# One group of small products moved from the middle of a layer to the border between two layers, in a fused delta-rule attention and MLP kernel

## The chip, the cores and the metric

The kernel runs on one core of one Trainium2 chip. The metric is the device time of one execution in microseconds (us); lower is better. Engines are called by the names that the profile gives them: PE is TensorE (matmuls), PEld its weight loads, DVE VectorE, ACT ScalarE, POOL GpSimd, SP the engine that issues most DMAs.

## The reference

For 4 sequences of 2048 tokens with 256 features the kernel computes one block with adaptive layer norm. Its first half is a gated delta rule in chunks of 64 tokens, its second half an MLP with ternary weights. Cut to what matters:

```python
h = layernorm(x) * (1 + ca) + sa
# attention: per head (4 heads, 64 wide), per chunk of 64 tokens, S is the state carried on
A     = inv(eye - A0)                    # A0 from keys x keys, strictly lower triangular
v_new = A @ v - (A @ wk) @ S             # the new values: "keys times old state" is in here
o     = rk_g @ S + intra @ v_new
S     = gamma_C * S + wk_g @ v_new
x = x + ga * (h + (alpha * o) @ Wr.T)
h = layernorm(x) * (1 + cb) + sb
h = silu(h @ w1.T * s1) * (h @ w2.T * s2)    # 256 -> 1024
h = gelu(h @ h1.T * s) ; h = gelu(h @ h2.T * s)   # 1024 -> 1024, twice
x = x + gb * (h @ w3.T * s3)                 # 1024 -> 256
```

All inputs and outputs are float32.

## The kernel before

**Tiling.** The state S ties the 32 chunks (`STEPS`) of a sequence together, so the kernel walks over chunks and treats all four sequences at once: a tile has 64 tokens of two sequences on its 128 partitions and the other pair beside them, 256 tokens in all (`TOK`). The MLP keeps features on the partitions and the 256 tokens along the free axis; its layers are called l1 (w1 and w2, 8 column blocks), l2 and l3 (the two 1024x1024 ones, 8 column blocks each, 16 matmuls per block), and y (w3). All weights stay on the chip. Activations are split into a high and a low part, which are multiplied with the same weights, one after the other (`act_hi`, `act_lo`; `xh`, `xl`).

**The attention's pieces** of one chunk, as names of the schedule: "start" (transposes of the normed tokens and keys), "values" (tokens times Ww), "gram" (keys times keys), "fs" and "expand" (the inverse of small blocks, VectorE), "pred" (keys times old state, for v_new), "u" (VectorE: values minus that product), "lead" (inverse times u, and queries times the old state), "join", "state" (the new state), "attn_out". Between attention and MLP of the same chunk stand "norm2" (VectorE: the second norm, tile `xn2`), "turn" (TensorE: transposes of `xn2`), "ln2" (ScalarE) and "parts" (VectorE: high and low part).

**What sets the order.** There is no scheduler. Lists written by hand give the order in which every engine meets the pieces: `alone` and `opening` for the first step, `second` and `third` for the next two, and `mixed` for steps 3 to 33 (of which 24 run in a hardware loop of 12 unrolled steps). Each engine walks the same list (`walk`, line 364) and issues, at each name, what this engine has to do for it. A name in the list thus sets a place in the queue of every engine that has code for it. Engines synchronise by semaphores that are waited for in front of the instruction.

A step n of `mixed` works on several chunks: l3 and y belong to step n-1, l1 and l2 to the chunk of step n, and an entry with 1 or 2 as its third number to a chunk ahead (`a = n + ahead`). So the order within a step is: transposes for the next chunk, l3 with its insertions, y, l1, "lead", l2 with its insertions.

**The lines that matter here.**
- TensorE, "pred" (lines 1318 to 1327, matmul L1325): for 4 pairs of sequence and head pair, 2 halves of the tokens and 2 heads, one product of a 64x64 block of the turned keys `rT` with a 64x64 block of `state`: 16 matmuls, each on a quarter of the array, into the columns 0 to 255 of both banks of `duo[0]`. It waits for the constants and for `hT_ready` and `rT_ready` of the chunk ahead (`begun`, line 384), since the transposes of that chunk lie in `duo[0]` until ScalarE and VectorE have copied them out.
- VectorE, "u" (lines 932 to 936): `v[p]` minus that product, written to `v[p]`; it sets `u_ready`, for which "lead" waits (line 1388).
- TensorE, "gram" (L1316, also 16 products on quarters of the array, into `duo[1]`), "values" (L1304, full array), "turn" (L1440, four transposes on the full array; it waits for `xn2_ready`, line 1437).
- TensorE, y (`last_layer`, L1235) and l1 (`layer`, L1163). The first l1 block waits for `xl_ready` and for VectorE's reading of `mlp[0]` (`y_mid[0]`, line 1177), the second for that of `mlp[1]` (line 1179).
- "lead" (L1136, L1142, then L1129, L1120) and "state" (L1420, L1422): groups of small products on quarters of the array, between l1 and l2 and inside l2.

Of the kernel before, what the change touches and what calls it, by code (L numbers as in the profile page):

```python
# [1 line left out]

# [104 lines left out]
def adaln_block(nc, x, wts, wv, wr, wmod, cT, scales, s3, decay, const, out):  # L107
    with ExitStack() as ctx:
        def sb(name, shape, dt=F32, c=ctx):
            return c.enter_context(nc.sbuf_tensor(name, [P] + list(shape), dt))  # L110

        def sem(name):
            return ctx.enter_context(nc.semaphore(name))

        def sems(name, n):
            return [sem(f"{name}{i}") for i in range(n)]

        main(nc, ctx, sb, sem, sems, x, wts, wv, wr, wmod, cT, scales, s3, decay, const, out)


def main(nc, ctx, sb, sem, sems, x, wts, wv, wr, wmod, cT, scales, s3, decay, const, out):
# [88 lines left out]
    gram = sb("gram", [2, NP, C])  # L210
    intra = [sb(f"intra{i}", [2, NP, C]) for i in range(2)]
# [28 lines left out]
    y = sb("y", [NB, D])  # L240
# [43 lines left out]
    def listed(first, columns, between):  # L284
# [4 lines left out]

    mixed = listed([("rg", 0, 0), ("start", 0, 1)], late + layers[:2 * HK], {  # L290
        ("l3", 0): [("norm2", 0, 0)],
        ("l3", 1): [("values", 0, 1), ("pred", 0, 0), ("gram", 0, 1), ("turn", 0, 0), ("intra", 0, 1), ("u", 0, 0)],
# [6 lines left out]
        ("l1", 7): [("lead", 0, 0), ("far", 0, 1), ("stats", 0, 2)],  # L299
        ("l2", 0): [("old", 0, 0), ("norm", 0, 2)],  # L300
        ("l2", 1): [("keys", 0, 0)],
# [1213 lines left out]
```

## Time and profile before

| | |
|---|---|
| median of 3 runs | 1745.33 us (1743.48 to 1747.3) |
| profiled execution, span from its first to its last instruction | 1742.3 us |
| profiled execution, its own device time | not given apart from the span; the three runs stand 1.2 to 5.0 us above the span |
| TensorE matmuls busy | 1716.0 us, 98% of the span |
| VectorE, ScalarE, GpSimd busy | 64%, 55%, 34% |
| HBM traffic | 18 GB/s over the span |

The span is what the trace covers; a run's time has the launch and the end in it as well. A matmul's "busy" time overlaps with that of the next (each lasts 0.28 us by the trace and the next starts 0.11 us later), so on TensorE it is the distance between starts that tells how fast work is issued. In the timelines a row can stand for several instructions of one line in a row (xcount); its time is the start of the first. Float32 products on quarters of the array leave two records each, so a group of 16 products is a row of x32.

### The profile page before, as it was taken

What the parts mean: (1) busy time and instruction counts of PE and PEld (TensorE: products, weight loads), DVE (VectorE), ACT (ScalarE), POOL (GpSimd) and SP (SyncE); (2) the same over time, 40 slices, a digit from 0 to 9 for tenths busy, and PEclk for the clock granted to TensorE, in tenths of its full rate; (3) what the DMA queues carried; (4) which work ended last, traced back from release to release, by engine and by line L of the source; (5) the groups of instructions that cost most, each with busy time, mean ns of one, the idle gap of its engine ahead of it and who ended that gap; (6) DMA issues with size and microseconds to landing.
All of it is one profiled execution on the core that took longest, in us unless ns stands there. A gap on an engine that the chain in (4) does not pass through costs nothing.

```text
span 1742.3 us, 60528 instructions
## 1 busy us (share of the span) xinstructions
PE 1716.0 (98%) x25488; PEld 1651.6 (95%) x25488; DVE 1115.4 (64%) x3041; ACT 963.3 (55%) x2249; POOL 593.5 (34%) x694
## 2 busy tenths in 40 slices
PE   8799999999999999999999999999999999999999
PEld 5698999999999999999999999999999999999998
DVE  5677666666666666676666676666666666666432
ACT  4664555555555555555555555555555555565554
POOL 3544333343333343333243333243233243243101
PEclk8899999999999999999999999999999999999999
DMA  8101000000000000000000000000000000000000
GB/s 291 68 14 33 12 23 23 18 20 11 24 23 23 18 20 11 24 23 24 17 21 15 20 23 23 20 17 19 16 23 23 21 17 21 14 23 17 8 3 12
DMA packets 37356, 47.08 MB, mean 27 GB/s; under 512 B 9236, under 2 KB 29336, under 8 KB 37080
## 3 DMA queue, kind: packets, MB, share of 16 engines
q1 hardware_dynamic: 35088, 40.75, 8.4%
q8 instruction: 206, 3.38, 0.8%
q10 hardware_dynamic: 1992, 2.38, 0.5%
q14 instruction: 70, 0.57, 0.1%
HBM read 22.53 MB, written 8.39 MB: 18 GB/s over the span
## 4 chain that ended last, share of the span: by engine, by line
PE 93%; DVE 1%; issue 1%; POOL 1%; ACT 1%; DVEq 0%; POOLq 0%
PE mlp L1163 64%; PE mlp L1235 6%; PE solo L1163 3%; PE duo L1431 3%; PE solo L1304 3%; PE solo L1136 2%; PE duo L1352 1%; PE duo L1129 1%; PE duo L1420 1%; PE solo L1440 1%; PE duo L1124 1%; PE duo L1325 1%; PE solo L1146 1%; PE duo L1422 1%; PE duo L1316 1%
## 5 line engine op out<-in xcount | busy, mean ns | idle before, releaser
L1163 PE MATMUL mlp<-act_hi,w_hi 128*128 128x256 f32 x4096 | 968.0, 283 | 1.1 <-POOL act_lo L668 0.6
L1163 PE MATMUL mlp<-act_lo,w_hi 128*128 128x256 f32 x4096 | 945.2, 277 | 0.0
L1163 PEld LDWEIGHTS mlp<-act_hi,w_hi 128*128 128x128 f32 x4096 | 770.1, 188 | 9.8 <-POOL act_lo L668 1.3
L1163 PEld LDWEIGHTS mlp<-act_lo,w_hi 128*128 128x128 f32 x4096 | 770.4, 188 | 0.8
L805 ACT ACTIVATE full<-mlp,scale_sb 128x256 f32<-128x256 f32 x512 | 246.4, 481 | 553.7 <-PE mlp L1163 553.5
L895 DVE TENSOR_TENSOR act_lo<-full,act_hi 128x256 fp32r<-128x256 f32 x512 | 240.2, 469 | 321.7 <-ACT act_hi L806 319.1
L668 POOL TENSOR_TENSOR act_lo<-full,act_hi 128x256 fp32r<-128x256 f32 x256 | 186.6, 735 | 501.9 <-ACT act_hi L795 501.9
L806 ACT ACTIVATE act_hi<-mlp,scale_sb 128x256 fp32r<-128x256 f32 x512 | 242.6, 474 | 0.0
L1163 PE MATMUL mlp<-xh,w_hi 128*128 128x256 f32 x768 | 190.8, 286 | 3.5 <-issue 3.0
L1163 PE MATMUL mlp<-xl,w_hi 128*128 128x256 f32 x768 | 189.8, 282 | 0.0
L607 POOL TENSOR_TENSOR rstd<-ve,minus_half 128x2 f32<-128x2 f32 x64 | 49.1, 768 | 331.7 <-DVE ve L844 331.3
L1014 DVE SCALAR_TENSOR_TENSOR full<-mlp,scale_sb,gate 128x256 f32<-128x256 f32 x192 | 92.8, 484 | 99.2 <-ACT gate L790 96.8
L1163 PEld LDWEIGHTS mlp<-xh,w_hi 128*128 128x128 f32 x768 | 145.9, 190 | 5.1 <-issue 4.2
L790 ACT ACTIVATE gate<-mlp,scale_sb 128x256 f32<-128x256 f32 x192 | 91.0, 474 | 107.7 <-PE mlp L1163 107.7
L1163 PEld LDWEIGHTS mlp<-xl,w_hi 128*128 128x128 f32 x768 | 146.2, 190 | 0.0
L1235 PE MATMUL mlp<-w_hi,act_hi 128*128 128x256 f32 x512 | 118.2, 277 | 0.0
L1235 PE MATMUL mlp<-w_hi,act_lo 128*128 128x256 f32 x512 | 118.1, 276 | 0.0
L607 POOL TENSOR_TENSOR rinv<-ssm,minus_half 128x8 f32<-128x8 f32 x32 | 52.8, 1650 | 182.2 <-DVE ssm L873 182.2
L795 ACT CAST act_hi<-full 128x256 fp32r<-128x256 f32 x256 | 101.7, 397 | 10.6 <-DVE full L1014 10.6
L1235 PEld LDWEIGHTS mlp<-w_hi,act_hi 128*128 128x128 f32 x512 | 96.1, 188 | 0.1
L1235 PEld LDWEIGHTS mlp<-w_hi,act_lo 128*128 128x128 f32 x512 | 96.1, 188 | 0.0
L779 ACT ACTIVATE h<-solo,sbm,cb 128x64 f32<-128x64 f32 x256 | 84.0, 438 | 0.3 <-PE solo L1440 0.3
(179 smaller groups left out, 2679.9 us busy)
## 6 DMA issues: line engine op xcount, KB each, us to landing
w_raw<-in_wts SPq DMA_DIRECT2D x22, 512.0 KB, 5.0
kg<-r SPq DMA_DIRECT2D x64, 126.0 KB
xin<-in_x SPq DMA_DIRECT2D x62, 128.0 KB
out_y<-y SPq DMA_DIRECT2D x62, 128.0 KB, 2.5
step_and_inv<-square_t SPq DMA_DIRECT2D x56, 64.0 KB, 2.0
wmod_sb<-in_wmod ACTq DMA_DIRECT2D x1, 1024.0 KB, 9.1
kg<-last SPq DMA_DIRECT2D x64, 2.0 KB
last<-r SPq DMA_DIRECT2D x64, 2.0 KB, 1.7
```

Source lines behind the costliest of these rows:

```text
L607: pool.tensor_tensor(dst[:], src[:], minus_half[:, 0:src.shape[1]], ALU.pow).then_inc(done, 1)
L668: pool.tensor_tensor(act_lo[0][:, k, :], full[k % 3][:], act_hi[0][:, k, :].bitcast(F32), ALU.subtract).then_inc(l_ready[0], 1)
L779: ins = act.activation(h2[:].rearrange("p k b n -> p (k b n)")[:, cols], solo[1][:, cols], ACT.Identity, bias=sbm[:, k, b:b + 1], scale=cb ...
L790: act.activation(gate[k % 2][:], gated[k % 3][:, 0:TOK], ACT.Silu, scale=scale_sb[:, 0, k:k + 1]).then_inc(l_act[0], 1)
L795: act.copy(act_hi[0][:, j, :], full[j % 3][:]).then_inc(l1_hi, 1)
L805: act.activation(full[k % 2][:], mlp[k % 2][:, 0:TOK], ACT.Gelu, scale=s)
L806: act.activation(act_hi[layer % 2][:, k, :], mlp[k % 2][:, 0:TOK], ACT.Gelu, scale=s).then_inc(l_act[layer], 1)
L895: dve.tensor_tensor(act_lo[layer % 2][:, k, :], full[k % 2][:], act_hi[layer % 2][:, k, :].bitcast(F32), ALU.subtract).then_inc(l_ready[la ...
L1014: dve.scalar_tensor_tensor(full[k % 3][:], up, s, gate[k % 2][:], ALU.mult, ALU.mult).then_inc(prod_ready, 1)
L1163: mm = pe.matmul(dst, *general_ops, start=is_first and i == 0, stop=is_last and i == 1)
L1235: mm = pe.matmul(mlp[k][:, 0:D], *ops, start=j == 0 and i == 0, stop=j == HK - 1 and i == 1)
L1304: mm = pe.matmul(solo[0][:, b * D:(b + 1) * D], hT[:, kt, b, :], wv_sb[:, kt, :], start=kt == 0, stop=kt == KT - 1)
```

## The change

One list is edited. In `mixed`, "pred" and "u" leave the place behind l3's second column and stand at the end of what follows l3's last column, behind both halves of y and so in front of l1. The lists of the first three steps are as before. The file also lost 15 blank lines at its top: line L1325 of before is L1310 of after, and so on for all.

```diff
     mixed = listed([("rg", 0, 0), ("start", 0, 1)], late + layers[:2 * HK], {
         ("l3", 0): [("norm2", 0, 0)],
-        ("l3", 1): [("values", 0, 1), ("pred", 0, 0), ("gram", 0, 1), ("turn", 0, 0), ("intra", 0, 1), ("u", 0, 0)],
+        ("l3", 1): [("values", 0, 1), ("gram", 0, 1), ("turn", 0, 0), ("intra", 0, 1)],
...
-        ("l3", 7): [("parts", 0, 0), ("silu", 0, 0), ("y", 0, 0), ("y", 1, 0)],
+        ("l3", 7): [("parts", 0, 0), ("silu", 0, 0), ("y", 0, 0), ("y", 1, 0), ("pred", 0, 0), ("u", 0, 0)],
```

TensorE at the old place, before: values (L1304), pred (L1325, `state` and `rT`), gram (L1316), turn (L1440), then l3's third column.

```order
L1163 MATMUL mlp<-act_lo,w_hi 128x256
L1300 REGISTER_ALU
L1304 MATMUL solo<-wv_sb,hT 128x256 x4
L1325 MATMUL duo<-state,rT 64x64 x16
L1316 MATMUL duo<-rT 64x65 x16
L1440 MATMUL solo<-con,xn 128x128 x4
L1163 MATMUL mlp<-act_hi,w_hi 128x256
```

The same place after the change (line numbers 15 lower):

```order
L1148 MATMUL mlp<-act_lo,w_hi 128x256
L1285 REGISTER_ALU
L1289 MATMUL solo<-wv_sb,hT 128x256 x4
L1301 MATMUL duo<-rT 64x65 x16
L1425 MATMUL solo<-con,xn 128x128 x4
L1148 MATMUL mlp<-act_hi,w_hi 128x256
```

The 16 products of pred are gone from between values and gram.

TensorE at the border from y (L1235) to l1 (L1163 with `xh` and `xl`), before:

```order
L1235 MATMUL mlp<-w_hi,act_hi 128x256
L1235 MATMUL mlp<-w_hi,act_lo 128x256
L1163 MATMUL mlp<-xh,w_hi 128x256
L1163 MATMUL mlp<-xl,w_hi 128x256
L1163 MATMUL mlp<-xh,w_hi 128x256
```

And after the change:

```order
L1220 MATMUL mlp<-w_hi,act_hi 128x256
L1220 MATMUL mlp<-w_hi,act_lo 128x256
L1310 MATMUL duo<-state,rT 64x64 x16
L1148 MATMUL mlp<-xh,w_hi 128x256
L1148 MATMUL mlp<-xl,w_hi 128x256
```

The 16 products, on quarters of the array, now stand between two layers on the full array.

VectorE at the same border, before: the two halves of y (L1024, L1026) and the first product of l1 (L1014):

```order
L1024 TENSOR_TENSOR y<-mlp,mods 128x256
L1026 TENSOR_TENSOR y<-y,x_0 128x256
L1024 TENSOR_TENSOR y<-mlp,mods 128x256
L1026 TENSOR_TENSOR y<-y,x_0 128x256
L1010 ISA
L1014 SCALAR_TENSOR_TENSOR full<-mlp,scale_sb,gate 128x256
```

And after, with u (L921, was L936):

```order
L1009 TENSOR_TENSOR y<-mlp,mods 128x256
L1011 TENSOR_TENSOR y<-y,x_0 128x256
L1009 TENSOR_TENSOR y<-mlp,mods 128x256
L1011 TENSOR_TENSOR y<-y,x_0 128x256
L921 TENSOR_TENSOR v<-v,duo 128x2x4x64
L995 ISA
L999 SCALAR_TENSOR_TENSOR full<-mlp,scale_sb,gate 128x256
```

The subtraction has moved behind the two halves of y; it stood behind "intra" (L930) before. ScalarE, GpSimd and SP have the same order before and after.

## Rows read from the trace of the kernel before

**Rows 1.** the page's head and its part 1, busy time of each engine
```profile
span 1742.3 us, 60528 instructions
...
PE 1716.0 (98%) x25488; PEld 1651.6 (95%) x25488; DVE 1115.4 (64%) x3041; ACT 963.3 (55%) x2249; POOL 593.5 (34%) x694
```

**Rows 2.** waits, whole run; columns: engine, line, awaited, us in total, times, longest
```profile
PEld duo L1325 <- issue: 9.6, 29, 0.3
...
PE solo L1440 <- DVE xn L1000: 2.2, 2, 1.9
```

**Rows 3.** all waits of TensorE from 230 to 1600 us
```profile
PE duo L1120 <- issue: 0.7, 2, 0.4
PE mlp L1163 <- issue: 0.3, 1, 0.3
```

**Rows 4.** one period: busy us by engine, then clock, DMA share, GB/s
```profile
1000.00:1052.00 52.00, 52.00 (x798) 50.60 (x797) 34.42 (x94) 28.95 (x70) 18.06 (x21) 1.00 0.08 20
```

**Rows 5.** TensorE's timeline, lead; start, length, line, operation, xcount [idle before]
```profile
1032.73 0.28 PE L1163 MATMUL mlp<-xl,w_hi 128*128 128x256 f32 x1
1032.94 0.27 PE L1136 MATMUL solo<-v,diag 64*64 64x64 f32 x2
...
1033.04 0.23 PE L1136 MATMUL solo<-v,diag 64*64 64x64 f32 x2
...
1033.10 0.22 PE L1136 MATMUL solo<-v,diag 64*64 64x64 f32 x2
```

**Rows 6.** TensorE's timeline, small groups inside the second layer
```profile
1046.24 0.69 PE L1420 MATMUL duo<-intra,vn 64*64 64x64 f32 x32
1046.75 0.65 PE L1422 MATMUL duo<-vn,kg 64*64 64x64 f32 x32
1047.33 0.38 PE L1163 MATMUL mlp<-act_hi,w_hi 128*128 128x256 f32 x1
1047.55 0.28 PE L1163 MATMUL mlp<-act_lo,w_hi 128*128 128x256 f32 x1
```

**Rows 7.** TensorE's timeline, the old place
```profile
1009.05 0.69 PE L1325 MATMUL duo<-state,rT 64*64 64x64 f32 x32
1009.57 0.65 PE L1316 MATMUL duo<-rT 64*64 64x65 f32 x32
1010.15 0.66 PE L1440 MATMUL solo<-con,xn 128*128 128x128 f32 x4
```

**Rows 8.** TensorE's timeline, the new place
```profile
1025.06 0.28 PE L1235 MATMUL mlp<-w_hi,act_lo 128*128 128x256 f32 x1
1025.17 0.28 PE L1163 MATMUL mlp<-xh,w_hi 128*128 128x256 f32 x1
1025.29 0.28 PE L1163 MATMUL mlp<-xl,w_hi 128*128 128x256 f32 x1
```

**Rows 9.** TensorE's timeline, turn in step 31
```profile
1632.37 0.66 PE L1440 MATMUL solo<-con,xn 128*128 128x128 f32 x4
```

**Rows 10.** VectorE's timeline, same step, and step 31
```profile
1007.59 1.79 DVE L1000 SCALAR_TENSOR_TENSOR xn<-x,mv,rstd 128x256 f32<-128x256 f32 x2
...
1011.64 0.68 DVE L936 TENSOR_TENSOR v<-v,duo 128x512 f32<-128x512 f32 x1
...
1025.83 0.42 DVE L1026 TENSOR_TENSOR y<-y,x 128x256 f32<-128x256 f32 x1
1026.83 0.48 DVE L1014 SCALAR_TENSOR_TENSOR full<-mlp,scale_sb,gate 128x256 f32<-128x256 f32 x1 [0.58 <-ACT gate L790]
...
1631.36 0.87 DVE L1000 SCALAR_TENSOR_TENSOR xn<-x,mv,rstd 128x256 f32<-128x256 f32 x2
```

**Rows 11.** TensorE's timeline, the new place in another step
```profile
817.13 0.32 PE L1163 MATMUL mlp<-xh,w_hi 128*128 128x256 f32 x1
817.29 0.28 PE L1163 MATMUL mlp<-xl,w_hi 128*128 128x256 f32 x1
```

## The prediction

> **What bounds the kernel now.** I read the page's first part first: TensorE's matmuls are busy for 98% of the span, the next engine (VectorE) for 64% [rows 1]. Then the waits: over the whole run TensorE waited twice, 2.2 us in all, for the normed tokens `xn`, the operand that stands next to the moved work [rows 2]; but from 230 to 1600 us, which is the steady loop, its waits are 0.7 + 0.3 = 1.0 us altogether, none of them on another engine [rows 3]. A stretch of 52.00 us, one period, has it busy for 52.00 us at a granted clock of 1.00, the 2.4 GHz level [rows 4]. So the time of the loop is the sum of the distances between the starts of its matmuls, and nothing that another engine does counts unless it makes TensorE wait. What a reordering can change is the distance at the borders between kinds of matmul. So I then read TensorE's timeline at the old place, at the new one and at two places that look like the new one will [rows 5 to 8], and last the other engines' rows beside them.
>
> **The change part by part.** The moved group on TensorE is 16 products of 64x64, 32 records (L1325). They run as four quadrants side by side: four starts close together, then the next four 0.06 us later. In steady state that is 1033.04 to 1033.10 for such a quad [rows 5]; eight quads make 0.47 us. The first quad after a border is longer, 1032.94 to 1033.04, so 0.05 us on top; that is also how 16 products entered from another tile size come to take 0.51 us, 1046.24 to 1046.75 [rows 6].
>
> *The old place.* The order is values (full 128x128 array), pred (64x64), gram (64x64), turn (full). From pred's start to gram's start it is 0.52 us (1009.05 to 1009.57) [rows 7]. When pred goes, gram becomes the first small group after values: it takes over the border with values and the longer first quad (0.05). The border from gram to turn stays. Saved: 0.52 - 0.05 = 0.47 us per step, and no border.
>
> *The new place.* Before, the last matmul of y is followed by the first of l1, both on the full array: start 1025.06, next 1025.17, next 1025.29, so 0.23 us from the last y to the second of l1 [rows 8]. Now a small group stands between. The nearest rows for its two borders are those at which l1 hands over to the small products of the block "lead", and those at which a group of 16 hands back to the second layer. Entry: last full matmul 1032.73, first small one 1032.94, 0.21 us [rows 5]. Exit: 16 small products and the border behind them, 1046.75 to 1047.33, 0.58 us, and then 0.22 us more to the second full matmul, 1047.55 [rows 6]. So from the last y to the second matmul of l1 it will be 0.21 + 0.58 + 0.05 (longer first quad) + 0.22 = 1.06 us. Added: 1.06 - 0.23 = 0.83 us per step.
>
> *The net* is 0.83 - 0.47 = 0.36 us per step: the group itself costs the same in both places, and the 0.36 is one extra change from the full array to quadrants (0.09 + 0.05) and one extra change back (0.11 + 0.10), each against two full matmuls in a row. Where it comes from shows in the weight loads: before pred's first record they sat idle 9.6 us in 29 cases, 0.33 us each, waiting for nothing but issue [rows 2]. Between full matmuls the next weights are loaded under the running product; at a change of tile size they are not.
>
> Here the Trainium skill bears on it, in "TensorEngine Tiling (Array Packing)", section "Tiling Modes": changing the tiling mode, not only the tile, drains the TensorE. "TensorE: Matmul & The Clock Gate", section "Step-by-step: what each phase is for", puts the drain at some 128 cycles. As an estimate by these pages two drains at 2.4 GHz are 0.11 us per step, 3.0 us over 28 steps, where the rows of this trace give 0.36 us per step.
>
> *Count.* The list `mixed` rules steps 3 to 33; pred happens in steps 3 to 31. In steps 3 to 30 values and gram stand beside it: 28 x 0.36 = 10.1 us. In step 31 (n + 1 is past the end, so no values and no gram) pred stands alone between l3 and turn, and turn starts at 1632.37. Without pred it can start no earlier than `xn` is there, 1631.36 + 0.87 = 1632.23 [rows 9, 10]. So there at most 0.14 us is saved and 0.83 added; I take +0.75 us.
>
> *A small gain.* In eight of the thirty borders between y and l1 the second start is 0.15 to 0.16 us after the first instead of 0.12, as at 817.13 to 817.29 [rows 11]: I read it as a short wait for VectorE, which has only just read the bank `mlp[0]` that l1 writes. Pred gives it 0.6 us more. That goes: -0.3 us in all.
>
> *What lies beside.* Turn waits for `xn`. At the old place it starts at 1010.15, `xn` is ready at 1007.59 + 1.79 = 1009.38 [rows 7, 10]: 0.77 us to spare. After the change turn comes 0.47 us sooner, so 0.30 us are left; the tight starts of this trace come 0.06 to 0.14 us after `xn`. Over the 28 steps this distance hardly varies, and what leads to `xn` (l3's first column, ScalarE, VectorE) stands ahead of the change. So this wait stays hidden, but barely. VectorE's subtraction `u` (L936, 0.68 us [rows 10]) moves behind y. Y's last operation there ends at 1025.83 + 0.42 = 1026.25, the first product of l1 starts at 1026.83 [rows 10]: 0.58 us of space, and TensorE's l1 moves 0.83 us later against y, so 1.4 us for 0.68. Nothing is queued late behind it. Its reader, the own products in the block "lead", starts at 1032.94 [rows 5], six us later. The bank `duo[0]` is not written between. At the old place VectorE is relieved of 0.68 us, but TensorE waits for nothing there, so that brings nothing. The semaphores that pred waits for (turned tokens and keys of the next step) are waited for by values and gram too, and gram starts at 1009.57 [rows 7], 15 us before pred's new place. ScalarE, GpSimd and the DMA queues keep their order; they follow TensorE.
>
> *Bounds of the border.* The borders from y into a small group and from one into l1 are not in this trace. Lower end: nothing at either, a group costs its own 0.47 us, net 0 per step. Upper end: each border costs the whole 0.33 us for which the weight loads stand idle ahead of pred [rows 2], 0.66 per step, 18.5 us over 28 and 18.9 us with the two small terms. I take 0.36, from the rows of the border nearest in kind: full array to small group to full array [rows 5, 6].
>
> *Sum.* 10.1 + 0.75 - 0.3 = +10.6 us on the profiled span of 1742.3 us, 1752.9 us. The median of the runs, 1745.33 us, is 3.0 us above that span (launch and end around it, and the spread of 1743.5 to 1747.3); carried over, 1755.9 us, +0.6%. What a measurement of this kernel can tell from no change is about 0.2%, 3.5 us.
>
> **The rivals.**
> A (forecast): two extra mode borders per step, 1755.9 us. For it: no wait hides them.
> B, not slower: the border into and out of l1 is free. L1's matmuls are 0.12 us apart, y's 0.11 [rows 8], so something other than streaming spaces them; if that has slack to take up the weight load, the group costs 0.47 us in both places, and only the small gain stays: 1745.33 - 0.3 = 1745.0 us. It decides from the point at which entry and exit together cost under 0.12 us (3.5 us over 28). Against it: at the exit into l2 the gap is twice the normal, and the weights of l1 are loaded in the same way.
> C, half: each border costs only what the first start at an entry shows, 0.09 us: 0.18 x 28 + 0.75 - 0.3 = 5.5 us, 1750.8 us. Against it stand the second starts, 0.22 instead of 0.11 [rows 6]. The drain of the Trainium skill ("TensorEngine Tiling (Array Packing)", "Tiling Modes") points this way; with the estimate above it would be 3.0 + 0.75 - 0.3, so 1748.8 us.
> D, slower still: turn falls on `xn`. It begins when the 0.30 us left are used up; if `xn` came 0.77 us later than in this trace against TensorE, all of the 0.47 us saved at the old place would be lost in each step: 10.6 + 28 x 0.47 = 23.8 us, 1769.1 us. Against it: nothing ahead of `xn` changes.
> That the change does nothing is excluded by the order: pred stands behind y in each of these steps.
>
> **How the numbers follow.** A 0.80, C 0.08, D 0.05, B 0.07. A's own spread: the borders within 0.05 us (1.4 us over 28), and a median of few runs within some 2 us, so 1752 to 1759.5; the upper end of the border, 1764.2 us, is far from every row that I have. The range reaches a little into C: 1751.0 to 1760.0. Slower by over 0.2% are A, C and D: 0.93. B splits into same 0.05 and faster 0.02.
>
> **What would show it.** In the profile after: a step of 52.36 us; L1325's first record 0.21 us behind the last y; 1.06 us from the last y to l1's second matmul; gram's records 0.52 us from start to next group instead of 0.47; turn 0.30 us behind `xn` and no wait of TensorE on it; the weight loads idle 0.33 us ahead of gram in 28 cases. The forecast is wrong if the step stays at 52.0 us (B) or TensorE shows waits on VectorE at turn (D).

## The result, and the profile after

| | before | after |
|---|---|---|
| median, us | 1745.06 (4 runs, 1743.48 to 1747.3) | 1755.94 (4 runs, 1754.31 to 1757.68) |
| ratio | | 1.006, 95% interval 1.0046 to 1.0074 |
| span of the profiled execution, us | 1742.3 | 1753.7 |
| usual length of a step of the loop, us | 52.00 | 52.35 |

The kernel is 0.6% slower; 1755.9 us was forecast. "Usual length" is the median distance between the same transposes of two neighbouring steps, over 26 steps of the trace. (Lines of the kernel after are 15 lower: pred is L1310, gram L1301, turn L1425, the layers L1148, y L1220, u L921, `xn` L985.)

The head of the page and its part 1 answer to [rows 1]: TensorE's matmuls are still at 98%, and the other engines do the same work.

```profile
span 1753.7 us, 60528 instructions
...
PE 1725.9 (98%) x25488; PEld 1655.9 (94%) x25488; DVE 1115.8 (64%) x3041; ACT 963.4 (55%) x2249; POOL 593.0 (34%) x694
```

All waits of TensorE from 230 to 1600 us answer to [rows 3]. There is still none on another engine, so nothing new is late.

```profile
PE duo L1105 <- issue: 1.4, 3, 0.6
PE mlp L1148 <- issue: 0.6, 2, 0.4
```

One period, as in [rows 4]: from 1380.00 to 1432.34 us the step is closed, TensorE is busy throughout and its clock is the same 1.00.

```profile
1380.00:1432.34 52.34, 52.34 (x798) 50.75 (x797) 34.43 (x94) 28.94 (x70) 18.04 (x22) 1.00 0.08 20
```

TensorE's timeline at the old place, against [rows 7]: gram's 16 products now follow values and take 0.63 us to the start of turn (1383.21 to 1383.84), where it was 0.58 (1009.57 to 1010.15). That is the longer first quad, 0.05 us.

```profile
1381.39 1.89 PE L1289 MATMUL solo<-wv_sb,hT 128*128 128x256 f32 x8
1383.21 0.70 PE L1301 MATMUL duo<-rT 64*64 64x65 f32 x32
1383.84 0.66 PE L1425 MATMUL solo<-con,xn 128*128 128x128 f32 x4
```

The new place, against [rows 8]: from the last y to the second matmul of l1 it is 1398.74 to 1399.79, 1.05 us, where it was 0.23. The parts are 0.21 us into the group, 0.62 for the group and the way out of it, 0.22 to the second start of l1.

```profile
1398.74 0.28 PE L1220 MATMUL mlp<-w_hi,act_lo 128*128 128x256 f32 x1
1398.95 0.69 PE L1310 MATMUL duo<-state,rT 64*64 64x64 f32 x32
1399.57 0.38 PE L1148 MATMUL mlp<-xh,w_hi 128*128 128x256 f32 x1
1399.79 0.28 PE L1148 MATMUL mlp<-xl,w_hi 128*128 128x256 f32 x1
```

VectorE in the same step, against [rows 10]. `xn` is ready at 1381.75 + 1.80 = 1383.55, turn starts 0.29 us later. Behind y, u starts at once (1399.86) and ends at 1400.54; the next product still waits 0.80 us for ScalarE. So both spare times that the prediction counted on were enough: no wait reached TensorE.

```profile
1381.75 1.80 DVE L985 SCALAR_TENSOR_TENSOR xn<-x,mv,rstd 128x256 f32<-128x256 f32 x2
...
1399.52 0.42 DVE L1011 TENSOR_TENSOR y<-y,x 128x256 f32<-128x256 f32 x1
1399.86 0.68 DVE L921 TENSOR_TENSOR v<-v,duo 128x512 f32<-128x512 f32 x1
1401.34 0.48 DVE L999 SCALAR_TENSOR_TENSOR full<-mlp,scale_sb,gate 128x256 f32<-128x256 f32 x1 [0.80 <-ACT gate L775]
```

The weight loads by line; the last columns are the idle time before them and its cause. The 0.33 us of [rows 2] stayed with the place, not with pred: in each of the 28 steps they now stand before gram (10.5 us in all, with the first steps of the run), while pred at its new place has 0.13 us each time.

```profile
L1301 PEld LDWEIGHTS duo<-rT 64*64 64x64 f32 x992 | 17.7, 137 | 10.5 <-issue 10.4
L1310 PEld LDWEIGHTS duo<-state,rT 64*64 64x64 f32 x992 | 17.3, 134 | 4.1 <-issue 0.3
```

### The profile page after: what moved, and what is told of

It is laid out like the page before. It is cut to its first block, busy times and chain, and to the rows that moved or that the text cites. A ratio compares the mean times of both kernels' runs of the same rounds, so it can differ in the third digit from the quotient of the medians.

```text
span 1753.7 us, 60528 instructions
## 1 busy us (share of the span) xinstructions
PE 1725.9 (98%) x25488; PEld 1655.9 (94%) x25488; DVE 1115.8 (64%) x3041; ACT 963.4 (55%) x2249; POOL 593.0 (34%) x694
## 4 chain that ended last, share of the span: by engine, by line
PE 93%; DVE 2%; issue 1%; POOL 1%; ACT 1%; DVEq 0%; POOLq 0%
PE mlp L1148 64%; PE mlp L1220 6%; PE solo L1148 3%; PE duo L1416 3%; PE solo L1289 3%; PE solo L1121 2%; PE duo L1337 1%; PE duo L1114 1%; PE duo L1405 1%; PE solo L1425 1%; PE duo L1109 1%; PE duo L1301 1%; PE duo L1310 1%; PE solo L1131 1%; PE duo L1407 1%
## 5 line engine op out<-in xcount | busy, mean ns | idle before, releaser
L1148 PE MATMUL mlp<-act_hi,w_hi 128*128 128x256 f32 x4096 | 968.1, 283 | 1.2 <-POOL act_lo L653 0.6
L1148 PE MATMUL mlp<-act_lo,w_hi 128*128 128x256 f32 x4096 | 945.5, 277 | 0.2 <-issue 0.2
L1148 PEld LDWEIGHTS mlp<-act_hi,w_hi 128*128 128x128 f32 x4096 | 769.9, 188 | 10.0 <-POOL act_lo L653 1.4
L1148 PEld LDWEIGHTS mlp<-act_lo,w_hi 128*128 128x128 f32 x4096 | 770.2, 188 | 1.4 <-issue 0.4
L1148 PE MATMUL mlp<-xh,w_hi 128*128 128x256 f32 x768 | 193.0, 288 | 4.9 <-issue 3.8
L1148 PE MATMUL mlp<-xl,w_hi 128*128 128x256 f32 x768 | 189.3, 283 | 0.0
L1148 PEld LDWEIGHTS mlp<-xh,w_hi 128*128 128x128 f32 x768 | 145.7, 190 | 8.0 <-issue 4.6
L1148 PEld LDWEIGHTS mlp<-xl,w_hi 128*128 128x128 f32 x768 | 145.8, 190 | 0.0
L1220 PE MATMUL mlp<-w_hi,act_hi 128*128 128x256 f32 x512 | 118.2, 277 | 0.0
L1220 PE MATMUL mlp<-w_hi,act_lo 128*128 128x256 f32 x512 | 118.0, 276 | 0.0
L1220 PEld LDWEIGHTS mlp<-w_hi,act_hi 128*128 128x128 f32 x512 | 96.1, 188 | 0.1
L1220 PEld LDWEIGHTS mlp<-w_hi,act_lo 128*128 128x128 f32 x512 | 96.1, 188 | 0.0
```

Source lines behind the costliest of these rows:

```text
L1148: mm = pe.matmul(dst, *general_ops, start=is_first and i == 0, stop=is_last and i == 1)
L1220: mm = pe.matmul(mlp[k][:, 0:D], *ops, start=j == 0 and i == 0, stop=j == HK - 1 and i == 1)
```

## The experiments

The theory is that only the number of borders between full-array and quarter-array products counts: one such group more between full-array matmuls costs 0.36 us per step, wherever it is and however many products it holds. The rivals were the place of u on VectorE, something special about the border of y and l1, and a cost that goes with the products displaced. All kernels are built on the one before. The ratio is against runs of the kernel before that were taken beside them (medians 1745.84 to 1747.81 us). "Step" is the usual distance between the same transposes of two neighbouring steps in the trace; two values stand where the steps fall into two groups.

| kernel | median, us | ratio (95%) | step, us |
|---|---|---|---|
| u alone behind y | 1748.45 | 1.001 (1.0001 to 1.002) | 52.00 |
| pred behind gram | 1746.81 | 0.9999 (0.9989 to 1.0009) | 52.00 |
| pred inside l3 | 1756.62 | 1.006 (1.0041 to 1.008) | 52.44 and 52.49 |
| pred in two halves, both moved | 1770.79 | 1.0133 (1.0114 to 1.0151) | 52.78 and 52.83 |
| one half moved, one not | 1761.01 | 1.0081 (1.006 to 1.0101) | 52.40 and 52.46 |
| pred left out | 1732.41 | 0.9923 (0.9907 to 0.994) | 51.53 and 51.60 |
| pred issued twice | 1770.84 | 1.0149 (1.0132 to 1.0166) | 52.87 and 52.93 |
| small groups ahead of values | 1764.37 | 1.011 (1.0093 to 1.0127) | 52.59 |
| turn ahead of the small groups | 1764.51 | 1.0094 (1.0067 to 1.0122) | 52.58 and 53.12 |
| gram ahead of values, pred inside l3 | 1771.61 | 1.0132 (1.0112 to 1.0151) | 52.69 to 53.26 |
| attn_out one column later | 1749.19 | 1.0005 (0.9996 to 1.0014) | 52.04 and 52.12 |

### Which half of the edit costs

u alone behind y:

```diff
-        ("l3", 1): [("values", 0, 1), ("pred", 0, 0), ("gram", 0, 1), ("turn", 0, 0), ("intra", 0, 1), ("u", 0, 0)],
+        ("l3", 1): [("values", 0, 1), ("pred", 0, 0), ("gram", 0, 1), ("turn", 0, 0), ("intra", 0, 1)],
...
-        ("l3", 7): [("parts", 0, 0), ("silu", 0, 0), ("y", 0, 0), ("y", 1, 0)],
+        ("l3", 7): [("parts", 0, 0), ("silu", 0, 0), ("y", 0, 0), ("y", 1, 0), ("u", 0, 0)],
```

> Only VectorE's subtraction u moves behind y; pred stays behind l3's second column. Border theory: TensorE's order is that of before and it waits for nothing, so the period stays 52.00 us and the time within 0.1% of before, 1745 us. Rival (VectorE's place for u is what costs): the period grows to about 52.34 us, 1755 us.

The usual step is the same to the nanosecond. Its time is 0.1% above before (1.9 us), at the edge of what the runs can tell and not explained; the profiled execution, with a span of 1742.1 us, was the fastest of the ten and cannot settle it. In the step, VectorE's half of the change costs nothing; a closed period of this kernel reads:

```profile
1367.73:1419.73 52.00, 52.00 (x798) 50.60 (x797) 34.43 (x95) 28.94 (x69) 18.07 (x21) 1.00 0.08 20
```

Pred behind gram:

```diff
-        ("l3", 1): [("values", 0, 1), ("pred", 0, 0), ("gram", 0, 1), ("turn", 0, 0), ("intra", 0, 1), ("u", 0, 0)],
+        ("l3", 1): [("values", 0, 1), ("gram", 0, 1), ("pred", 0, 0), ("turn", 0, 0), ("intra", 0, 1), ("u", 0, 0)],
```

> Pred changes places with gram, next to it, so it moves but crosses no border between full-array and quarter-array products. Border theory: period 52.00 us, time as before, 1745 us. Rival (any later pred costs, or pred must not stand right ahead of a full-array group): 52.1 us or more.

52.00 us and a ratio of 0.9999: moving pred without crossing a border is free.

### The two terms apart

Pred left out (in `mixed`, u does not wait for it either and subtracts what lies in the bank, so the result is no longer that of the block):

```diff
-        ("l3", 1): [("values", 0, 1), ("pred", 0, 0), ("gram", 0, 1), ("turn", 0, 0), ("intra", 0, 1), ("u", 0, 0)],
+        ("l3", 1): [("values", 0, 1), ("gram", 0, 1), ("turn", 0, 0), ("intra", 0, 1), ("u", 0, 0)],
```

> In the list mixed the 16 products of pred are left out of the computation and u subtracts what lies in the bank. This measures what the old place gives back. By my sum: 0.47 us per step, no border goes: period 51.53 us, 28 x 0.47 + 0.1 = -13.3 us, 1731.8 us. Rival (a border goes too, or turn then waits for xn and eats part): 51.17 us in the one case, 51.6 us or more in the other.

The usual step is 51.53 us (51.60 in those in which a stretch of l2 runs at the slower pace told below): the old place gives back 0.47 us, as summed, and the time fell by 13.4 us, where 13.3 were expected. Values, gram and turn stand as in the kernel after:

```profile
1363.22 1.89 PE L1305 MATMUL solo<-wv_sb,hT 128*128 128x256 f32 x8
1365.04 0.70 PE L1317 MATMUL duo<-rT 64*64 64x65 f32 x32
1365.67 0.66 PE L1441 MATMUL solo<-con,xn 128*128 128x128 f32 x4
```

Pred issued twice (the second issue, behind y, first waits for u_ready):

```diff
+                        if k == 3:
+                            pe.wait_ge(u_ready, a)
...
-        ("l3", 7): [("parts", 0, 0), ("silu", 0, 0), ("y", 0, 0), ("y", 1, 0)],
+        ("l3", 7): [("parts", 0, 0), ("silu", 0, 0), ("y", 0, 0), ("y", 1, 0), ("pred", 3, 0)],
```

> Pred stays in the old place and is issued a second time behind y, into the same bank, with the same result. This measures what the new place costs by itself. By my sum: 0.83 us per step in 29 steps: period 52.83 us, +24 us, 1769 us. Together with the run in which pred is left out it must give the change: 0.83 - 0.47 = 0.36. Rival (the cost is in the interplay of the two places): the two do not add up.

25.0 us more, 24 expected. From the last y (1412.03) to the second of l1 (1413.08) it is 1.05 us against 0.23: the second group costs 0.82. The step shows 0.87 to 0.93; the rest, 0.05 to 0.11, is no border but the pace of other stretches, told below. So 0.82 - 0.47 = 0.35 us, and the change is the sum of its two halves.

```profile
1412.03 0.28 PE L1235 MATMUL mlp<-w_hi,act_lo 128*128 128x256 f32 x1
1412.23 0.69 PE L1327 MATMUL duo<-state,rT 64*64 64x64 f32 x32
1412.86 0.38 PE L1163 MATMUL mlp<-xh,w_hi 128*128 128x256 f32 x1
1413.08 0.28 PE L1163 MATMUL mlp<-xl,w_hi 128*128 128x256 f32 x1
```

### Place and number of products

Pred inside l3: behind its fifth column instead of behind y (and, as in the change, gone from behind values).

```diff
-        ("l3", 4): [("fs", 2, 1)],
+        ("l3", 4): [("fs", 2, 1), ("pred", 0, 0), ("u", 0, 0)],
```

> Pred and u stand behind l3's fifth column instead, between full-array matmuls of one layer. Border theory: one extra change of array mode and back, 0.09 + 0.05 + 0.11 + 0.11 = 0.36 us, period 52.34 to 52.36 us, some 10 us over before, 1755 us, as for the change. Rival (the border of y and l1 is special: y's bank hand-over, l1's wider spacing of 0.12 us): the period differs from that of the change by 0.05 us or more.

The time is that of the change, ratio 1.006. The step is 0.09 to 0.14 us longer than that of the change, which by my own words speaks for the rival; but the border itself shows the same numbers as behind y (0.206 in, 0.148 out, 0.221 to the second start, medians over 26 steps, from the starts in the trace), and the surplus lies in l2: in every second step the 32 matmuls ahead of "state" run at a slower pace, and in 11 of the 13 others the 32 behind it.

Pred in two halves of 8 products, one inside l3, one behind y, none left behind values:

```diff
-                        for q, c, e in blocks:
+                        for q, c, e in {0: blocks, 1: blocks[:8], 2: blocks[8:]}[k]:
...
-        ("l3", 4): [("fs", 2, 1)],
+        ("l3", 4): [("fs", 2, 1), ("pred", 1, 0)],
...
-        ("l3", 7): [("parts", 0, 0), ("silu", 0, 0), ("y", 0, 0), ("y", 1, 0)],
+        ("l3", 7): [("parts", 0, 0), ("silu", 0, 0), ("y", 0, 0), ("y", 1, 0), ("pred", 2, 0), ("u", 0, 0)],
```

> Pred in two halves of 8 products, one behind l3's fifth column and one behind y. Border theory: the same 16 products with two extra borders, 0.72 us per step, period 52.70 us, 28 x 0.70 + 1 = +21 us, 1766 us. Rival (the cost goes with the products displaced, not with the borders): 52.35 us, 1756 us.

One half moved, one not: with the same last line, but the first half left behind values:

```diff
-        ("l3", 1): [("values", 0, 1), ("pred", 0, 0), ("gram", 0, 1), ("turn", 0, 0), ("intra", 0, 1), ("u", 0, 0)],
+        ("l3", 1): [("values", 0, 1), ("pred", 1, 0), ("gram", 0, 1), ("turn", 0, 0), ("intra", 0, 1)],
```

> 8 of pred's 16 products stay behind l3's second column, 8 go behind y. Border theory: one extra border, whatever the number of products behind it: period 52.34 to 52.36 us, +10 us, 1755 us, like the whole change. Rival (the cost goes with the products displaced): half of it, 52.17 us, 1750 us.

Same products, two extra borders: 52.78 to 52.83, so 0.78 to 0.83 per step and 1.33%, about twice the change. One half moved: 52.40 to 52.46, the full price of one border and not half of it (52.17). Counted from the starts at the borders alone, without the rest of the step, it is 0.72 us for the two halves and 0.35 for the one. These are the runs that rule out "the cost goes with the products". A half behind y takes 0.39 us instead of 0.62 and has the same 0.21 before and 0.22 behind:

```profile
1413.61 0.28 PE L1235 MATMUL mlp<-w_hi,act_lo 128*128 128x256 f32 x1
1413.82 0.46 PE L1325 MATMUL duo<-state,rT 64*64 64x64 f32 x16
1414.21 0.39 PE L1163 MATMUL mlp<-xh,w_hi 128*128 128x256 f32 x1
1414.43 0.28 PE L1163 MATMUL mlp<-xl,w_hi 128*128 128x256 f32 x1
```

Both came out higher than expected: 24 us over before instead of 21, and 15 instead of 10. The pace of other stretches has a part in it, and so have stalls (5 to 6 us over 26 steps, against 1.7 before); with one half moved, TensorE also waited twice for GpSimd's `act_lo`, 0.9 us in all.

### How near turn may come, and a surprise

Small groups ahead of values:

```diff
-        ("l3", 1): [("values", 0, 1), ("pred", 0, 0), ("gram", 0, 1), ("turn", 0, 0), ("intra", 0, 1), ("u", 0, 0)],
+        ("l3", 1): [("pred", 0, 0), ("gram", 0, 1), ("values", 0, 1), ("turn", 0, 0), ("intra", 0, 1), ("u", 0, 0)],
```

> Pred and gram stand ahead of values instead of behind it, so the quarter-array group hands over to values (float32, starts 0.215 us apart) and values to turn. As many borders as before. The wide spacing of values should hide the second gap of an exit (0.22 us for the second start): 0 to 0.1 us less per step, period 51.9 to 52.0 us, 1742 to 1745 us. Rival (a hand-over from values to turn costs something of its own, as the 0.31 us do behind attn_out): 52.0 to 52.1 us.

A clear miss: 1.1% slower, 52.59 us. The wide spacing of values hides nothing: the second start of values comes 0.320 us after the first instead of 0.215, and the borders together cost 0.04 us more than before, as the rival had it. Far more comes from l3 and y, which run slower. 54 matmuls of l3 take 1396.75 - 1390.39 = 6.36 us, 0.118 us each:

```profile
1390.39 0.28 PE L1163 MATMUL mlp<-act_hi,w_hi 128*128 128x256 f32 x1
...
1396.75 0.28 PE L1163 MATMUL mlp<-act_hi,w_hi 128*128 128x256 f32 x1
```

In the kernel before the same 54 take 1017.01 - 1010.88 = 6.13 us, 0.1135 each:

```profile
1010.88 0.28 PE L1163 MATMUL mlp<-act_hi,w_hi 128*128 128x256 f32 x1
...
1017.01 0.28 PE L1163 MATMUL mlp<-act_hi,w_hi 128*128 128x256 f32 x1
```

From the first of l3's matmuls behind turn to the start of l1 it is 15.16 us instead of 14.61: 0.55 us per step for 128 matmuls. With the 0.04 of the borders that is the surplus.

Turn ahead of the small groups:

```diff
-        ("l3", 1): [("values", 0, 1), ("pred", 0, 0), ("gram", 0, 1), ("turn", 0, 0), ("intra", 0, 1), ("u", 0, 0)],
+        ("l3", 1): [("values", 0, 1), ("turn", 0, 0), ("pred", 0, 0), ("gram", 0, 1), ("intra", 0, 1), ("u", 0, 0)],
```

> Turn stands right behind values, ahead of pred and gram, so it comes some 1.1 us sooner than in the kernel before and must wait for the normed tokens xn, with which its slack was 0.75 us. This tests how close turn may come: my sum gives 0.04 us for the other borders and 0.4 to 0.5 us of wait, period 52.5 us, +14 us, 1759 us, with turn's start 0.06 to 0.14 us behind the end of xn. Rival (xn does not bind): 52.04 us, 1746 us. It also tests the surprise of the run with the small groups first, in which l3 ran at 0.118 us per matmul instead of 0.113: if that comes from values next to turn as such, l3 is at 0.118 here too (+0.55 us more, 53.05); if quarter-array products ahead of l3 set the pace back, it is at 0.113.

Here TensorE waits for `xn`, and the view says so:

```profile
1390.96 1.89 PE L1304 MATMUL solo<-wv_sb,hT 128*128 128x256 f32 x8
1393.18 0.66 PE L1440 MATMUL solo<-con,xn 128*128 128x128 f32 x4 [0.33 <-DVE xn L1000]
1393.77 0.70 PE L1325 MATMUL duo<-state,rT 64*64 64x64 f32 x32
1394.28 0.65 PE L1316 MATMUL duo<-rT 64*64 64x65 f32 x32
```

VectorE's row of the same step ends at 1391.33 + 1.79 = 1393.12:

```profile
1391.33 1.79 DVE L1000 SCALAR_TENSOR_TENSOR xn<-x,mv,rstd 128x256 f32<-128x256 f32 x2
```

Turn starts 0.06 us behind `xn`, and so it is in all steps (0.054 to 0.056 us). From the last start of values to turn it is 0.71 us instead of 0.22: 0.49 us of wait per step. So turn may come within 0.06 us of `xn` before it costs; the change left 0.29. The usual step is 52.58, where 52.5 was expected; in 8 of 26 steps l3 ran at the slow pace, and these have 53.11 or more. Neither reading of the pace that was on trial (values next to turn, or a reset by small products) holds as a rule.

Gram ahead of values, pred inside l3 (gram also waits for hT_ready, since it writes a bank that ScalarE has just read):

```diff
-        ("l3", 1): [("values", 0, 1), ("pred", 0, 0), ("gram", 0, 1), ("turn", 0, 0), ("intra", 0, 1), ("u", 0, 0)],
+        ("l3", 1): [("gram", 0, 1), ("values", 0, 1), ("turn", 0, 0), ("intra", 0, 1)],
...
+        ("l3", 4): [("fs", 2, 1), ("pred", 0, 0), ("u", 0, 0)],
```

> As the run with the small groups first (gram, values, turn), but pred and u stand behind l3's fifth column. If a group of quarter-array products sets the pace of the following full-array matmuls back, l3's columns 3 to 5 run at 0.118 us per matmul and columns 6 to 8 and y at 0.113: 80 matmuls x 0.0045 = 0.36 us less than in that run (52.58) for a border that costs 0.36, so period 52.6 us, 1763 us. If the pace is set by something else in the step (the other engines, or l3 as a whole), it is 0.118 or 0.113 throughout: 52.95 us or 52.4 us.

1771.6 us, 8 us more than expected, and my idea of a reset fails. Of 25 steps, l3's third to fifth column ran slow in 15 and fast in 10. Behind pred, the 10 fast ones stayed fast, but of the 15 slow ones only 5 became fast. A group of small products between does not set the pace back as a rule. Which ones became fast is not random: the 5 all lie in steps of one parity, the 10 that stayed slow all in steps of the other. Part of the surplus is another wait: without pred ahead of it, turn comes too soon again, 0.37 us behind the last start of values instead of 0.22.

### A cheaper border elsewhere

attn_out one column later:

```diff
-        ("l2", 6): [("attn_out", 0, 0), ("residual", 0, 2)],
+        ("l2", 6): [("residual", 0, 2)],
+        ("l2", 7): [("attn_out", 0, 0)],
```

> Built on the kernel before, with another border: the output projection attn_out (float32, full array) stands behind l2's eighth column, next to the transposes of the next step, instead of behind its seventh. In the trace of before, going back from it to the layer costs 0.028 + 0.306 us for two starts instead of 0.226, and the 16 matmuls behind it run 0.118 us apart instead of 0.113: 0.11 + 0.07 = 0.18 us per step that this could save, if the hand-over to the transposes is free, as between values and turn. Border theory: period 51.82 us, -5 us, 1741 us. If the slow pace goes over to the 32 matmuls of l3's first two columns (0.14 us): 51.96 us, 1745 us. Rival: the later x1 holds up VectorE and TensorE waits in the next step: above 52.0 us.

No gain: 1.0005. The hand-over to the transposes is free, as hoped (1371.20 to 1372.93 is 8 x 0.216 us):

```profile
1371.20 1.89 PE L1432 MATMUL duo<-wr_turned,o_state 128*128 128x256 f32 x8
1372.93 0.60 PE L1288 MATMUL duo<-con,h 128*128 128x128 f32 x4
```

But so was the old one, and the sum above had it wrong. Before, it is 0.334 us from the last start of attn_out to the second start of l2 (0.028 + 0.306), and 0.216 of that is the spacing of attn_out itself; the 0.118 left are one step of l2's slower pace. There was no border price of 0.11 us to save:

```profile
1051.08 1.89 PE L1431 MATMUL duo<-wr_turned,o_state 128*128 128x256 f32 x8
1052.62 0.47 PE L1163 MATMUL mlp<-act_hi,w_hi 128*128 128x256 f32 x1
1052.93 0.28 PE L1163 MATMUL mlp<-act_lo,w_hi 128*128 128x256 f32 x1
```

The 0.07 us that the slow matmuls behind attn_out cost could have been saved, but the pace ate it: in 15 of 26 steps the 48 matmuls between "state" and attn_out run at 0.118 us (32 of them ran at 0.113 before), and in every second step the 32 ahead of "state" do. There is no wait of TensorE on another engine from 230 to 1600 us. So none of the orders tried beats the kernel before.

## Why the prediction was right

**The bound.** The prediction said that TensorE's starts set the time and no other engine does. That is right: from 230 to 1600 us no wait of TensorE names another engine, before [rows 3] or after. Where an order did make TensorE wait (turn ahead of the small groups), the wait was there at once, in the row and in the time.

**The old place.** 0.47 us forecast, 0.47 measured by leaving pred out. (Among the signs, the prediction gave gram's length as 0.52 us instead of 0.47; it left the way out to turn out of both. The difference, 0.05 us, is what the rows show: 0.63 against 0.58.)

**The new place.** 0.83 forecast from the borders of "lead" and of the second layer [rows 5, 6], 0.82 measured. The weakest step, that the borders of y and l1, which the trace did not show, cost what others do, held: 0.206 us in and 0.148 + 0.221 out are the medians at y and l1, and the other borders between the full array and quarters have the same to 0.003 us.

**The net.** 0.36 forecast; from one usual step to the other it is 52.347 - 52.000 = 0.347 us. The mechanism was right, and so was its size.

**Shown, and not shown.** That it is the border and not the products, the place or u is shown by the runs with one half, with two halves, inside l3 and with u alone. A rival that I had not named is the precision: in this kernel the layers' operands have the type `float32r`, one record for each product, while the small products are plain float32, two records for each, so each border changes both. The trace of before tells the two apart. From a layer to values (float32 on the full array) the next start comes after 0.117 us, as between two matmuls of the layer, and the way back from attn_out costs nothing either, as shown above. From values to pred (float32 on both sides, another tile size) it is 0.309 us, of which 0.216 are the spacing of values: 0.093 more, the same as the 0.206 - 0.113 from y to pred. On the way out, gram to turn, float32 on both sides again, has the same 0.148 us as pred to l1. So the price goes with the tile size and not with the precision.

What happens inside TensorE at such a border stays open. That the weight load no longer hides is what I argued; no run took the tile size away and kept the products. The drain that the Trainium skill names ("TensorEngine Tiling (Array Packing)", "Tiling Modes") agrees in direction. By the 128 cycles that the Trainium skill gives for the last column to leave the array ("TensorE: Matmul & The Clock Gate", "Step-by-step: what each phase is for"), two drains at 2.4 GHz are an estimated 0.11 us. The 0.35 us measured are three times that. Rival C, which allowed 0.18 us per step, is excluded by the same 0.35, and so is B, which allowed nothing.

**Step 31.** I took +0.75 us for it, and the trace bears it out: turn comes 0.08 us earlier (0.14 at most was forecast) and 0.82 us are added behind y, 0.73 in all. It does not show in the distance between the turns of steps 31 and 32, which grew by only 0.27 us, because l3 of step 31 happened to run at the slower pace in the kernel before (15.15 us from its first start behind turn to l1) and at the usual pace after (14.70 us to pred):

```profile
1632.78 0.36 PE L1163 MATMUL mlp<-act_hi,w_hi 128*128 128x256 f32 x1
1647.93 0.28 PE L1163 MATMUL mlp<-xh,w_hi 128*128 128x256 f32 x1
```

```profile
1643.35 0.37 PE L1148 MATMUL mlp<-act_hi,w_hi 128*128 128x256 f32 x1
1658.05 0.69 PE L1310 MATMUL duo<-state,rT 64*64 64x64 f32 x32
```

In step 32 it is the other way round (14.61 us before, 15.16 after), so the two cancel.

**What the forecast left out.** In each execution single small products of TensorE are late, with "issue" named and no engine, as here in the kernel after:

```profile
358.46 0.25 PE L1105 MATMUL duo<-inv,cross 64*64 64x32 f32 x2 [0.61 <-issue]
```

Gaps that are over 0.03 us longer than the median at the same place, most of them ahead of small products, sum up to 1.7 us over 26 steps in the profiled execution of before and 4.2 us in that of after; over all kernels here it is 1.7 to 6.2, in no order that I can see.

**The sum.** The steps give 28 x 0.347 + 0.73 - 0.2 = 10.2 us (the 0.2 is the small gain, forecast as 0.3: the eight late second starts in l1 are gone), against 10.6 forecast and 10.9 measured between the medians. The two profiled spans differ by 11.4 us: ahead of step 3, where nothing was changed, the kernel after happened to be 1.7 us shorter, and stalls and slow stretches added 2.7 us over 26 steps. So that the forecast met the median to 0.1 us is luck; that it met it to 2 us is not.

## What to carry to other kernels

On a kernel whose TensorE never waits, count the borders between full-array matmuls and groups on parts of the array: each group that stands alone costs a fixed price (here 0.35 us per step, the same for 8 and for 16 products), so put small groups side by side, and test a move by what it neighbours, not by how far it goes. Read entry and exit from a place in the same trace where such a group already stands, to the second start behind it. When you read a border, take off the spacing that the matmuls ahead of it have anyway. And compare the length of a closed step in the trace: it tells 0.05 us per step apart, which is 1.4 us over 28 steps, where the medians scatter by some 2 us.

## What I had not expected

**Two paces of the same matmul.** Full-array matmuls with 256 columns run, within one stretch between two other groups, at 0.1133 or at 0.1178 us apart, mostly one or the other for the whole stretch, with the same instructions and the clock granted in full. In the kernel before only the 16 matmuls behind attn_out are slow in the usual step; the change left that so. In the one with the small groups ahead of values all of l3 was slow. This second effect reached 0.55 us per step, more than the border itself, and most of the other orders tried had some of it. It follows a pattern: with pred inside l3, with both halves moved and with attn_out one column later, the 32 matmuls ahead of "state" were slow in exactly every second step, and with turn ahead of the small groups all 8 slow l3 lay in steps of one parity. The kernel's steps alternate between two sets of buffers (index `p`); whether that is the reason no run tells. What chooses the pace is open: slow stretches came behind the float32 groups on the full array, but also where none was near, and a small group between did not reliably end them.

**The first product behind values.** The 0.33 us of idle weight loads [rows 2] belong to the hand-over from values, whose matmuls are 0.216 us apart, not to small groups as such; ahead of pred behind y it is 0.13. As the upper end of my range it was far too wide, and for the wrong reason.
